# Queries' layer norm taken tile by tile, with x tiles 1 to 3 loaded from ScalarE's queue and the first weights in two halves on SyncE's

## What is computed

```python
def _layernorm(x, axis=-1, eps=1e-05):
    m = jnp.mean(x, axis=axis, keepdims=True)
    v = jnp.var(x, axis=axis, keepdims=True)
    return (x - m) / jnp.sqrt(v + eps)
...
q = (hidden_states @ q_proj_w.T).reshape(B, Q, NUM_HEADS, HEAD_DIM)
q = rmsnorm(q, q_norm_w)
...
x = x + _L0_xattn_ref(_layernorm(x, axis=-1), ctx_4096, ...)
x = x + _L0_attn_ref(_layernorm(x, axis=-1), ...)
x = x + _L0_ffn_ref(_layernorm(x, axis=-1), ...)
```

## Time and profile before

| | |
|---|---|
| median of 3 runs | 2276.41 us (2275.97 to 2276.83) |
| the profiled execution's own time | 2275.54 us |
| its span (first to last instruction) | 2273.6 us |
| TensorE busy | 2249.8 us, 99% of the span |
| VectorE, ScalarE, GpSimd busy | 84%, 57%, 69% |
| granted TensorE clock | 1.00 |

### The profile page before, as it was taken

How to read it: one execution, slowest core, us unless ns; L and a number is a source line. 1 busy time by engine, 2 the same in 40 slices (tenths; PEclk the granted TensorE clock), 3 DMA queues, 4 the chain that set the end, 5 groups by cost and what they waited for, 6 DMA issues and landing times. The chain is left out here.

```text
span 2273.6 us, 46237 instructions
## 1 busy us (share of the span) xinstructions
PE 2249.8 (99%) x19084; PEld 1614.4 (71%) x19084; DVE 1909.2 (84%) x2574; ACT 1296.4 (57%) x2073; POOL 1571.3 (69%) x1079
## 2 busy tenths in 40 slices
PE   8999999999999999999999999999999999999998
PEld 4567777777777777777777777777777645555554
DVE  7768888888888888888888888888889957988887
ACT  7755555555555555555555555555456646767673
POOL 0328888888888888888888888888888601433432
PEclk9999999999999999999999999999999999999999
DMA  9421111110110101101101110010000373222210
GB/s 317 136 80 32 28 27 29 36 29 20 28 31 28 28 28 34 31 20 36 28 20 30 29 28 28 28 35 22 12 30 26 116 224 112 84 66 84 94 48 20
DMA packets 107710, 122.86 MB, mean 54 GB/s; under 512 B 9582, under 2 KB 76398, under 8 KB 107502
## 3 DMA queue, kind: packets, MB, share of 16 engines
q1 hardware_dynamic: 104462, 110.44, 15.7%
q0 software_dynamic: 3040, 9.47, 1.4%
HBM read 99.94 MB, written 19.96 MB: 53 GB/s over the span
## 5 line engine op out<-in xcount | busy, mean ns | idle before, releaser
L188 POOL TENSOR_TENSOR p_l<-S,p_h 128x1792 f16<-128x1792 f32 x126 | 422.6, 3354 | 140.3 <-ACT p_h L520 140.3
L620 DVE SCALAR_TENSOR_TENSOR S<-pS,rk,mask 128x256 f32<-128x256 f32 x832 | 355.4, 478 | 98.4 <-PE pS L289 54.1
L289 PE MATMUL p_acc<-w_l,ctx_h 128*128 128x256 f16 x1536 | 418.7, 273 | 0.0
L289 PE MATMUL p_acc<-w_h,ctx_l 128*128 128x256 f16 x1536 | 418.7, 273 | 0.0
L289 PE MATMUL p_acc<-w_h,ctx_h 128*128 128x256 f16 x1536 | 418.6, 273 | 0.0
L630 DVE TENSOR_REDUCE mx<-S 128x256 f32<-128x3328 f32 x63 | 376.9, 5983 | 2.2
L289 PE MATMUL p_acc<-ctx_h,w_h 128*128 128x400 f16 x1016 | 337.6, 332 | 0.9 <-PEq L945 0.9
L289 PE MATMUL p_acc<-ctx_l,w_h 128*128 128x400 f16 x1016 | 337.6, 332 | 0.0
L289 PE MATMUL p_acc<-ctx_h,w_l 128*128 128x400 f16 x1016 | 336.9, 332 | 0.0
L656 DVE TENSOR_TENSOR S<-S,pO 128x1792 f32<-128x1792 f32 (+1 forms) x128 | 240.9, 1883 | 87.2 <-PE pO L358 87.2
L766 POOL TENSOR_TENSOR sq_l<-sq_f,sq_h 128x400 f16<-128x400 f32 (+1 forms) x256 | 242.6, 948 | 85.9 <-ACT sq_h L496 85.9
(11 more groups left out here) (333 smaller groups left out, 5225.7 us busy)
## 6 DMA issues: line engine op xcount, KB each, us to landing
ctx_p<-ctxT_dram SPq DMA_DIRECT2D x42, 458.0 KB, 3.6
s_wst<-winG_dram SPq DMA_DIRECT2D x8, 1536.0 KB, 6.8
q_wst<-wqT_dram SPq DMA_DIRECT2D x8, 1024.0 KB, 6.9
o_scratch<-o_st SPq DMA_DIRECT2D x32, 256.0 KB, 2.7
s_wst<-winG_dram SPq DMA_DIRECT2D x8, 1024.0 KB, 5.3
m_wost<-woutG_dram SPq DMA_DIRECT2D x8, 1024.0 KB, 5.4
qh<-q_hi_scratch SPq DMA_DIRECT2D x64, 64.0 KB, 1.9
ql<-q_lo_scratch SPq DMA_DIRECT2D x64, 64.0 KB, 2.0
```

Of the source, the lines that this page charges most:

```text
L188: eng.tensor_tensor(p_l[:, s % 2, t0:t1, :], S[:, s % 2, t0:t1, :], p_h[:, s % 2, t0:t1, :], ALU.subtract).then_inc(pl_ok, 1)
L289: mm = pe.matmul(out, x, y, start=first and j == 0, stop=final and j == 2)
L620: ins = dve.scalar_tensor_tensor(out=S[:, s % 2, t, :].rearrange("p (r q) -> p r q", r=REP), in0=bank[:, t % 2, :].rearrange("p (r q) -> p ...
```

## The change

Four edits. (1) Queues: SyncE's queue loads tile 0 of x, then the group 0 weights as two transfers of half the size, each with a semaphore of its own, then the norm weights; ScalarE's queue loads tiles 1 to 3 of x ahead of ScalarE's other work. (2) The layer norm is taken tile by tile on VectorE, ScalarE and TensorE, with the functions for one tile. Tile 0 goes first; VectorE normalises tile 1 between the low parts of the weights' two halves, and tiles 2 and 3 after them; TensorE turns tile t + 1 in the middle of tile t's matmuls of group 0. (3) In the last state-space group GpSimd makes m_yl of tile 2 before the power of tile 0, and no longer after it. (4) ScalarE takes the root of tile 1 (`deviation(1)`) before the copy f_hT of tile 0 (`normed_turned(0)`), and no longer after it. The old functions `vector`, `vector_turned`, `scalar`, `scalar_turned` and `tensor` of `LayerNorm` are taken out.

```diff
         @block.sync
         def _(sp):
-            for t in range(TT):
-                sp.dma_start(xs[:, t, :], x[t * P:(t + 1) * P, :]).then_inc(x_in[t], 16)
+            sp.dma_start(xs[:, 0, :], x[0:P, :]).then_inc(x_in[0], 16)
+            for h in range(2):
+                rows = slice(HID // 2 * h, HID // 2 * h + HID // 2)
+                sp.dma_start(wst[:, 0, KC // 2 * h:KC // 2 * h + KC // 2, :],
+                             wqT[rows, 0:512].rearrange("(k p) c -> p k c", p=P)).then_inc(w_in[h], 16)
             sp.dma_start(nw[:, :], norm_w).then_inc(ctx_in[NCH - 1], 16)
...
-            body(0, 0)
-            sp.wait_ge(w_in[0], 16)
+            sp.wait_ge(w_in[1], 16)
+            sp.wait_ge(x_in[TT - 1], 16)
             body(0, 1)
...
         @block.tensor
             pe.wait_ge(idt, 2)
-            ln.tensor(pe)
+            ln.tile_turned(pe, 0)
...
                         if g == t == 0 and k in (0, KC // 2):
                             pe.wait_ge(w_lo, 1 + k // (KC // 2))
+                        if g == 0 and k == KC // 2 and t + 1 < TT:
+                            ln.tile_turned(pe, t + 1)
...
             def split(pair, j):
-                wait(act, w_in[j], 16 * (pair + 1))
+                wait(act, w_in[j], 16 * (pair + 1 + j))
...
             def first_split(h):
-                act.wait_ge(w_in[0], 16)
+                act.wait_ge(w_in[h], 16)
...
+            for t in range(1, TT):
+                act.dma_start(xs[:, t, :], x[t * P:(t + 1) * P, :]).then_inc(x_in[t], 16)
             act.wait_ge(consts, 2)
             act.activation(root[:, :], eps[:, 0:1], ACT.Sqrt)
-            ln.scalar(act)
+            ln.tile_deviation(act, 0)
             first_split(0)
-            ln.scalar_turned(act, range(1))
+            ln.tile_high(act, 0)
             first_split(1)
-            ln.scalar_turned(act, range(1, TT))
+            for t in range(1, TT):
+                ln.tile_deviation(act, t)
+                ln.tile_high(act, t)
...
-            ln.vector(dve, x_in)
-            dve.wait_ge(ctx_in[NCH - 1], 16)
-            dve.tensor_tensor(nwp[:, :], nw[:, 0:1], nw[:, 1:2], ALU.mult).then_inc(consts, 1)
+
+            def normed(t):
+                dve.wait_ge(x_in[t], 16)
+                ln.tile_moments(dve, t)
+                ln.tile_normed(dve, t)
...
+            normed(0)
             first_split(0)
-            ln.vector_turned(dve, range(1))
+            ln.tile_low(dve, 0)
+            normed(1)
             first_split(1)
-            ln.vector_turned(dve, range(1, TT))
+            ln.tile_low(dve, 1)
+            for t in range(2, TT):
+                normed(t)
+                ln.tile_low(dve, t)
+            dve.wait_ge(ctx_in[NCH - 1], 16)
+            dve.tensor_tensor(nwp[:, :], nw[:, 0:1], nw[:, 1:2], ALU.mult).then_inc(consts, 1)
...
                 low(g, 1)
                 join_squares(g, 1)
+                low(g, 2)
                 tile_power(g, 0)
-                low(g, 2)
                 join_squares(g, 2)
...
                 deviation(0)
+                deviation(1)
                 normed_turned(0)
-                deviation(1)
                 deviation(2)
```

More of the change, by code:

```diff
@@ L847, in __init__ @@
             self.high = ctx.enter_context(nc.semaphore(f"{tag}_high"))
-    def vector(self, dve, x_in=None):
-        for t in range(TT):
[L852 to L863, removed]
     def tile_moments(self, dve, t):
@@ L898, in tile_low @@
                                  in1=th[:, :, cols], op0=ALU.mult, op1=ALU.subtract).then_inc(self.done, 1)
[L900 to L929, removed]
 def identity(pool, ident, sem):
```

## The result

The changed kernel takes 2279.86 us (22 runs, 2279.36 to 2280.22) against 2276.28 us for the kernel before (22 runs, 2274.7 to 2278.65) on the same chips: ratio 1.0016, 95% interval [1.001, 1.0022]. It is slower, by 3.6 us of medians, which is inside the 0.2% that I called no change. The two profiled executions differ by more: 2279.92 against 2275.54 us, spans 2278.1 against 2273.6.

What follows compares the result with a forecast made beforehand. TensorE, busy 99% of the span, was taken as the bound, so a later group 1 moves the end. Head +6.46 and tail -1.14 give +5.3 us on the median 2276.41: 2281.7 us, range 2279.0 to 2284.0.

Steps and rivals of the forecast that it cites:

- rival A: Group 0: the forecast itself, TensorE waits on the norm round through three engines; 2281.7 us, chance 0.67.
- Own time to median: Whole kernel: the median of before lies 0.87 us above its profiled time, so the forecast adds that to 2280.9.
- W: Start: time at which the first weight half is used, predicted 7.7 us, ends 5.4 and 9.6.
- The first matmul: Start of group 0 on TensorE: W + 2.97, at 10.7 us, 1.9 us earlier than before.
- The second low part: VectorE's low part of the second weight half, queued behind tile 1's norm: begins at W + 4.78.
- T1: Start of tile 1's transposes on TensorE, behind the wait for the second half's low part: W + 6.06.
- The round: Group 0, one tile's transposes to the next's through three engines: 4.07 us against TensorE's own 3.02.
- First turn and group 1: End of group 0: work queued behind tile 3's norm makes TensorE wait 1.9 and 1.1 us; group 1 at W + 22.81.
- Tail, ScalarE: Tail: the earlier root of tile 1 lets VectorE's chain to the end finish 1.14 us sooner.
- B: Loads: like rival A, but SyncE's queue is favoured, W = 5.4 to 6.5; 2279.4 us, chance 0.19.
- C: Group 0: no slower, norms of tiles 1 to 3 hide under TensorE's matmuls; 2276.1 us, chance 0.06.
- D: Group 0: pauses of 0.7 to 1.9 us keep TensorE at the slow pace; 2287.6 us, chance 0.08.

Runs made afterwards that it cites:

- tail_act: Kernel before with only ScalarE's root of tile 1 moved ahead of the copy f_hT of tile 0; 2275.05 us against 2276.18, ratio 0.9994.
- squares_early: Changed kernel with squares and roots of tiles 0 and 1 and tile 0's scaled product moved forward; 2276.98 us, ratio 1.0002.
- all_early: Changed kernel with x on SyncE's queue behind the weights, 24 added identity transposes, earlier squares, norms before low parts; 2273.32 us against 2275.97, ratio 0.9988.
- head_only: Changed kernel with the two tail edits (GpSimd's and ScalarE's order) undone, so only the new start; 2281.56 us, ratio 1.0024.
- one_queue: Changed kernel with x tiles 1 to 3 loaded by SyncE's queue behind the weights; 2278.31 us (one run).
- pe_busy: Changed kernel with 20 unused identity transposes ahead of tile 0's transposes and 16 behind; 2279.09 us (one run).
- norms_ahead: Changed kernel with norms of tiles 2 and 3 around the previous tile's low part, and tile 2 turned two chunks earlier; 2278.81 us (one run).
- before_best: Kernel before with ScalarE's tail root moved ahead of the copy, and 36 identity transposes before the first tile; 2274.22 us against 2275.97, ratio 0.9994.
- before_pe_busy: Kernel before with 36 unused identity transposes ahead of its own; 2275.68 us against 2276.11, ratio 0.9997.
- tail_pool: Kernel before with only GpSimd's m_yl of tile 2 moved ahead of the power of tile 0; 2276.11 us (one run).
- all_but_busy: Same as all_early but without the 24 identity transposes; 2274.4 us against 2276.82, ratio 0.9991.

## Why the prediction came out as it did

I forecast 2281.7 us and got 2279.86, within the range, but on the other side of the 4.55 us that part slower from the same: I had given slower 0.70 and the same 0.29. The mechanism (rival A, the ring through three engines) was right; terms of the sum were off, in this order:

- **Own time to median.** "The median of before is 0.87 above the profiled time", and I added that to the changed kernel too. This was the wrong step. The changed kernel has no such offset: its profiled 2279.92 is its median, and so is its profiled span (2278.1, the median of the 22). The profiled execution of before was a quick one: in three sets of 21 further runs (those beside tail_act, squares_early and all_early) the median span is 2274.2, 0.6 above the profiled 2273.6. Less the 2249.6 behind group 1 that is a group 1 at about 24.6 in a median execution. That the 0.6 lies in the head is inferred: the runs that read a granted clock of 1.00 have nearly the same medians (2274.1 to 2274.2), so it isn't the falls of the pace in the tail. The changed kernel's 22 runs lie within 0.9 us, where those of before spread over 4. Two profiles fit that: the slow pace ended at 15.5 us in head_only and about 14.3 in the changed kernel, and T2 is 17.49 and 17.50, since TensorE waits for the norm of tile 2 either way. So the wait that makes the kernel slower would also make its head steady; the runs agree, but the two profiles are all that show how.
- **W.** Predicted 7.7, measured 7.02. The sharing was about as assumed; what I had wrong is the rate, taken from before's 215 GB/s by 7.2 us. The changed kernel has 252, one_queue 250. That is -0.68 us. Why more passes isn't shown: the weights in two transfers, and the norm weights behind, are the differences that one_queue shares with it. The rate also varies by execution: 205 to 239 in the five profiles with the loads of before, 252 to 257 in the six with those of the changed kernel, 226 to 250 in the three on one queue.
- **The first matmul** at W + 2.97: measured W + 2.97 (9.99). **The second low part** at W + 4.78: W + 4.75. **T1** at W + 6.06: W + 6.03.
- **The round**, 4.07: measured 4.45 to T2 and 4.00 to T3. The first is longer because of the slow transposes: from T1 to q_th is 1.15, from T2 0.70, so 0.45 where 0.43 was predicted (0.47 at group 1 by pe_busy). That term was right in place and in size, and the round itself was 0.07 shorter than the 4.07 of the sum.
- **First turn and group 1** at W + 18.25 and W + 22.81 with the slow transposes: W + 18.12 and W + 22.67. The waits are 1.69 (predicted 1.9) and 0.87 (1.1). squares_early shows what hung on this order: 2.8 us, more than on the rounds (1.0 by norms_ahead; an estimate with the pace of the changed kernel is 8.45 - 6.04 - 0.48 - 0.15 = 1.8, the 0.15 for its two slower matmuls behind T1).
- **Tail, ScalarE** -1.14: measured -1.19, and -1.18 alone, in the profiles. By medians the changed kernel is 1.7 us below head_only; the falls of the pace that edit 4 very likely spares were no term of the sum. **Tail, GpSimd** 0: measured 0.

Summed by the profiles: 5.3 - 0.68 - 0.14 - 0.05 = 4.4 us, which is their difference. The difference of medians is 0.8 less. Of this the spans show 0.6, the quick execution of before; the remaining 0.2 lies outside the spans or between the sets of runs, and was not followed.

Of the rivals, B (W = 5.4) didn't happen, though its order can be had by writing it (one_queue). C needed rounds under 3.02 us. D did not occur in group 0 of the changed kernel, whose waits between its matmuls are 1.69 us at most, but the pace did come back slow after longer ones (2.70 us in all_early, 2.13 in before_best). What stays open in these runs is why an execution of one kernel has its weights or its fast pace a microsecond earlier than another; before_pe_busy kept one run in eleven at 2278.5, so the pace at the start isn't all of it.

## What to carry to other kernels

Work that was done while a transfer was awaited costs nothing; spread over the tiles, it becomes a chain from engine to engine, and what counts is that chain's length against the bounding engine's own work for a tile (4.07 against 3.02 here), and also what stands behind the chain's last link in each engine's list (2.8 us of squares). An earlier first matmul says little; look for the first moment from which the bounding engine never waits again, and compare kernels by it. And before adding a predicted difference to a median, ask whether the profiled execution is a typical one: two profiles of one head differed by 1.2 us here. The spans and granted clocks of all runs, set beside those of the profiled one, answer it.

## What the runs showed of the hardware

- **The moment at which TensorE's pace doubles differs between executions of one instruction list.** The kernel before, tail_act and tail_pool have the same list up to there, and the pace is the fast one from 13.25, from 15.11, and already ahead of 12.58. When TensorE began doesn't decide it: the first transposes start at 8.80, 9.12 and 9.30, and the last to start was the first to be fast. The changed kernel (about 14.3) and norms_ahead (16.01) differ likewise, with one list up to 12.88. The granted clock reads 1.00 in these stretches all the same; only the spacing of the matmuls shows it (0.43 against 0.22 us for 512 columns, 1.2 and 2.4 GHz).
- **The pace can fall back after a wait.** In tail_pool, after a wait of 2.11 us for the experts' choice, and here the granted clock shows it (clock is the third number from the end):

```profile
2258.00:2262.00 4.00, 2.09 (x14) 1.90 (x15) 3.74 (x13) 1.09 (x4) 0.00 (x0) 0.93 0.00 0
2262.00:2266.00 4.00, 4.00 (x17) 2.69 (x16) 2.77 (x10) 1.15 (x4) 0.00 (x0) 0.64 0.16 59
```

```profile
2259.86 0.33 PE L1991 MATMUL m_ab<-s_ident,f_w 128*128 128x128 f32 x1 [2.11 <-DVE f_w L2560]
...
2261.85 1.92 PE L1996 MATMUL p_acc<-f_bw,f_wT 128*128 128x512 f32 x2
```

The same two products take 1.02 us at the fast pace, and the stretch to the end was 1.0 us longer. In the profiled executions of head_only and of the kernel before the wait was also 2.11 and the pace stayed, so a fall doesn't follow in every execution. With edit 4 the wait is 0.93, and no profile of a kernel with that edit shows the fall there.

The mean granted clock of the other runs says how often a fall comes, though not where. All three profiled executions with a fall (tail_pool, all_early, before_best) read 0.999 and the other eleven 1.00. Runs at 0.999:

| kernel | wait in the tail | runs at 0.999 |
|---|---|---|
| before, four sets | 2.11 | 25 of 78 |
| head_only | 2.11 | 8 of 11 |
| before_pe_busy | 2.11 | 7 of 11 |
| after | 0.93 | 0 of 22 |
| tail_act | 0.93 | 2 of 11 |
| squares_early | 0.94 | 1 of 11 |
| all_early, all_but_busy | 0.93 | 1 of 11 each |
| before_best | 0.93 | 3 of 11 |

The one of all_early and one of the three of before_best were profiled, and their falls are at the start. head_only and the changed kernel differ in edits 3 and 4 alone: 8 of 11 against 0 of 22, and the eight are 0.85 us longer than the three, near the 1.0 of tail_pool. So edit 4 very likely takes away falls in the tail too, and is then worth more than its 1.2 us with this head; that they lie in the tail was seen in one profile only. Why head_only falls more often than the kernel before, with the same tail, isn't shown.

- **Transposes of float32 alone raised the pace**: 20 and 16 of the identity around tile 0's four, and the first product ran fast (pe_busy). The same held for 36 in front of the kernel before (before_pe_busy, spacing 0.22 from 12.31 on), and these took 6.04 us where 36 at the slow 0.217 would take 7.8, so the pace rose among them. In tail_pool, with no transpose added, the layer norm's own sixteen did it.
